# Router logits of twelve FFN tiles from four column tiles of 32, a copy and one product with a fixed 128x8 matrix

## The reference

```python
x = x + xattn(layernorm(x), ctx, ctx, pos, mask, Wq, Wk, Wv, Wo)   # RoPE, masked softmax
# the FFN, on xf = layernorm(x) as 2048 x 512
router_logits = xf @ gate_w.T            # gate_w is 8 x 512
routing = softmax(router_logits, axis=1) # 8 weights for each row
in_scale  = routing @ in_channel_scale   # 8 x 512
out_scale = routing @ out_channel_scale
out = (xf * in_scale) @ sign(weight).T * out_scale + bias
x = x + out
```

## Time and profile before

| | before |
|---|---|
| median of 3 runs | 1149.29 us (1148.65 to 1153.01) |
| the profiled execution, its time | 1149.49 us |
| its span, first to last instruction | 1147.7 us |
| PE busy | 98% of the span |
| PEld, DVE, POOL, ACT busy | 83%, 71%, 62%, 47% |
| granted TensorE clock, mean | 1.000 |

### The profile page before, as it was taken

One profiled execution on the slowest core, in us unless ns is written; L12 is line 12 of the kernel. 1 busy time (PEld: TensorE's weight loads), 2 busy tenths in 40 slices (PEclk: granted clock), 3 DMA queues, 4 the chain that ended last, 5 costly groups with the idle time before them and its releaser, 6 DMA issues.

```text
span 1147.7 us, 22887 instructions
## 1 busy us (share of the span) xinstructions
PE 1130.3 (98%) x7919; PEld 951.8 (83%) x7919; DVE 815.5 (71%) x1363; ACT 537.2 (47%) x1736; POOL 706.1 (62%) x586
## 2 busy tenths in 40 slices
PE   7999999999999999999999999999999999999998
PEld 6778888888888888888888888888888888888876
DVE  5876876767687766877767676677766767776566
ACT  4644444454444454444553435544444544445533
POOL 5855675555667556675665666566675656755544
PEclk9999999999999999999999999999999999999999
DMA  8323332333323222333422323233232232322200
GB/s 233 111 72 114 114 115 82 90 96 94 93 82 102 74 82 85 121 107 92 116 85 68 103 75 90 91 106 107 84 94 73 74 92 65 93 72 83 83 20 37
DMA packets 134339, 105.29 MB, mean 92 GB/s; under 512 B 10664, under 2 KB 108984, under 8 KB 134256
## 3 DMA queue, kind: packets, MB, share of 16 engines
q1 hardware_dynamic: 128848, 93.72, 27.8%
q10 hardware_dynamic: 4640, 8.40, 2.1%
q0 software_dynamic: 768, 2.10, 0.6%
HBM read 100.00 MB, written 4.19 MB: 91 GB/s over the span
## 4 chain that ended last, share of the span: by engine, by line
PE 91%; DVE 3%; issue 2%; DMA 1%; ACT 1%; POOL 1%; SPq 0%; DVEq 0%; ACTq 0%; POOLq 0%
PE chunk L1232 22%; PE chunk L1234 21%; PE chunk L1233 21%; PE duo_ps L1298 6%; PE o_ps L1321 3%; PE duo_ps L1221 2%; PE aux L1221 2%; PE duo_ps L1321 2%; PE chunk L1278 1%; PE o_ps L1280 1%; PE o_ps L1279 1%; PE chunk L1280 1%; PE o_ps L1278 1%; PE chunk L1279 1%; DVE swp L931 1%
## 5 line engine op out<-in xcount | busy, mean ns | idle before, releaser
L448 POOL TENSOR_TENSOR w_lo<-raw,w_hi 128x512 fp32r<-128x512 f32 x192 | 247.8, 1304 | 311.9 <-ACT w_hi L589 311.7
L931 DVE TENSOR_TENSOR swp<-chunk,sinT 64x512 f32<-64x512 f32 x320 | 220.3, 688 | 54.2 <-PE chunk L1234 33.4
L589 ACT ACTIVATE w_hi<-raw 128x512 fp32r<-128x512 f32 x192 | 116.4, 629 | 270.1 <-PE chunk L1234 203.8
L1232 PE MATMUL chunk<-xT_hi,w_hi 128*128 128x512 f32 x512 | 206.7, 404 | 0.6 <-POOL w_lo L448 0.6
L1234 PE MATMUL chunk<-xT_hi,w_lo 128*128 128x512 f32 x512 | 200.3, 391 | 0.0
L1233 PE MATMUL chunk<-xT_lo,w_hi 128*128 128x512 f32 x512 | 199.7, 390 | 0.0
L1232 PE MATMUL chunk<-wo_hi,oT_hi 128*128 128x512 f32 x496 | 196.8, 397 | 1.2 <-DVE oT_lo L865 1.2
L1234 PE MATMUL chunk<-wo_hi,oT_lo 128*128 128x512 f32 x496 | 193.5, 390 | 0.0
L1233 PE MATMUL chunk<-wo_lo,oT_hi 128*128 128x512 f32 x496 | 193.3, 390 | 0.0
L626 ACT ACTIVATE probs<-scores,neg_max 128x64 f32<-128x64 f32 x512 | 170.4, 337 | 41.2 <-DVE neg_max L887 41.2
L455 POOL TENSOR_TENSOR qT<-qT,swp 128x512 f32<-128x512 f32 x128 | 165.2, 1298 | 35.9 <-DVE qT L933 35.5
(11 more groups left out here) (271 smaller groups left out, 2033.5 us busy)
## 6 DMA issues: line engine op xcount, KB each, us to landing
raw<-in_L_xattn_Wq SPq DMA_DIRECT2D x128, 256.0 KB, 2.8
raw<-in_L_xattn_Wo SPq DMA_DIRECT2D x128, 256.0 KB, 2.7
raw<-in_L_xattn_Wk SPq DMA_DIRECT2D x32, 256.0 KB
raw<-in_L_xattn_Wv SPq DMA_DIRECT2D x32, 256.0 KB, 3.0
acc<-in_x ACTq DMA_DIRECT2D x14, 256.0 KB, 7.4
x_tile<-in_x SPq DMA_DIRECT2D x12, 256.0 KB, 2.9
c_tile<-in_ctx SPq DMA_DIRECT2D x12, 256.0 KB, 3.2
result<-y ACTq DMA_DIRECT2D x12, 256.0 KB, 2.0
```

The lines of the kernel that those rows point to most:

```text
L448: nc.gpsimd.tensor_tensor(lo, raw[:, r, :], hi.bitcast(F32), ALU.subtract).then_inc(wsplit_lo, 1)
L589: return nc.scalar.activation(dst, src, ACT.Copy)
L931: last = nc.vector.tensor_tensor(swp[to, k, :], bank[of, :], sinT[to, here], ALU.mult)
L1232: nc.tensor.matmul(bank, a_hi, b_hi, start=i == 0, stop=False)
```

## The change

In the twelve slots `t_logits` is replaced by two steps. `t_partials` makes four products whose stationary operand is 32 columns of the gate matrix (8 of them filled, 24 zeros) and whose moving operand is one 128x128 chunk of the transposed tile; chunk c goes to partitions 32c to 32c+31 of `aux`, so each product has a column tile of its own and none accumulates. ACT copies the 128x128 result to `partT`. `t_sum_partials` then makes one product with `partT` as stationary and the fixed 128x8 matrix `gate_pick` as moving operand, which sums the four partial results and gives the logits in the old layout. `t_partials` stands ahead of `probs_T`, `t_sum_partials` where `t_logits` stood. The copy stands on ACT between the weight splits and `pT_hi_split`. `last_tiles` keeps `t_logits`. At the start DVE sums four 8-column groups of the identity to make `gate_pick`, and ACT's one copy to `gateT` is 128x128 instead of 128x32.

```diff
@@ buffers
-        gateT = sb("gateT", [P, EC, NE])
+        gateT, gate_pick, partT = sb("gateT", [P, EC, 32]), sb("gate_pick", [P, NE]), sb("partT", [P, P])
@@ ScalarE
+            def partial_logits(f, b):
+                act.wait_ge(part_done, f + 1)
+                copy(b.partT, b.bank[:, 0:P]).then_inc(part_ok, 1)
...
                 split_hi(s, 4)
                 if s.odd:
                     split_hi(s, 5)
+                if s.ffn:
+                    partial_logits(f[0], in_slot)
                 pT_hi_split(s, 0)
                 pT_hi_split(s, 1)
...
-                copy(gateT[:, :, :], by_chunk(GATE_BANK)[:, :, 0:NE]).then_inc(gate_ok, 1)
+                copy(gateT[:, :, :], by_chunk(GATE_BANK)[:, :, 0:32]).then_inc(gate_ok, 1)
@@ VectorE, first_positions
+                dve.wait_ge(ident_ok, 2)
+                nc.vector.tensor_reduce(gate_pick[:, :], ident[:, :].rearrange("p (c e) -> p e c", c=EC)[:, 0:NE, :], AX.X, ALU.add).then_inc(pick_ok, 1)
                 dve.wait_ge(pos_in, 16)
@@ TensorE
+            def t_partials(f, b):
+                pe.wait_ge(fn_T, f + 1)
+                for c in range(EC):
+                    last = nc.tensor.matmul(b.bank[32 * c:32 * c + 32, 0:P], gateT[:, c, :], b.tile_T[:, bass.ts(c, P)],
+                                            start=True, stop=True)
+                last.then_inc(part_done, 1)
+
+            def t_sum_partials(f, b):
+                pe.wait_ge(part_ok, f + 1)
+                nc.tensor.matmul(b.bank[:, 0:NE], b.partT, gate_pick[:, :], start=True, stop=True).then_inc(lg_done, 1)
...
                 project(s, 0)
                 if not s.odd:
                     project(s, 1)
+                if s.ffn:
+                    t_partials(f, in_slot)
                 probs_T(s, 0)
                 probs_T(s, 1)
...
                 if s.ffn:
-                    t_logits(f, in_slot)
+                    t_sum_partials(f, in_slot)
                 project(s, 1 if s.odd else 2)
```

More of the change, by code:

```diff
@@ L144, in attention_ffn, with __init__ @@
         class FfnBuffers:
-            def __init__(self, stat, mv, var, rstd, bank, tile, tile_T, route, routeT, rexp, rmax, rsum, rrec, xs_hi, xs_lo, y):
+            def __init__(self, stat, mv, var, rstd, bank, tile, tile_T, route, routeT, rexp, rmax, rsum, rrec, xs_hi, xs_lo, y, partT):
+                self.partT = partT
                 self.stat, self.mv, self.var, self.rstd = stat, mv, var, rstd
@@ L156, in attention_ffn @@
         in_slot = FfnBuffers(f_stat[:, :], f_mv[:, :], f_var[:, :], f_rstd[:, :], aux[:, :], f_tile[:, :], fT[:, :], route[:, :], routeT[:, :], rexp[:, :],
-                             rmax[:, :], rsum[:, :], rrec[:, :], xs_hi[:, :], xs_lo[:, :], y[:, :])
+                             rmax[:, :], rsum[:, :], rrec[:, :], xs_hi[:, :], xs_lo[:, :], y[:, :], partT[:, :])
         at_end = [FfnBuffers(s_stat[:, p, :], s_mv[:, p, :], s_var[:, p:p + 1], s_rstd[:, p:p + 1],
@@ L163, in attention_ffn @@
                              xT_hi[:, p, E:2 * E], xT_lo[:, p, E:2 * E],
-                             (cosT if p < 2 else sinT)[:, bass.ts(p % 2, E)]) for p in range(PAIRS)]
+                             (cosT if p < 2 else sinT)[:, bass.ts(p % 2, E)], None) for p in range(PAIRS)]
         assert QT % 2 == 0
@@ L199, in attention_ffn @@
         fn_tr, fn_T, lg_done, rm_ok, re_ok, rr_ok = (sem(n) for n in ("fn_tr", "fn_T", "lg_done", "rm_ok", "re_ok", "rr_ok"))
+        part_done, part_ok, pick_ok = sem("part_done"), sem("part_ok"), sem("pick_ok")
         rt_ok, rt_tr, rt_hi, rt_lo = (sem(n) for n in ("rt_ok", "rt_tr", "rt_hi", "rt_lo"))
@@ L1374, in t_logits @@
                 for c in range(EC):
-                    last = nc.tensor.matmul(b.bank[:, 0:NE], b.tile_T[:, bass.ts(c, P)], gateT[:, c, :],
+                    last = nc.tensor.matmul(b.bank[:, 0:NE], b.tile_T[:, bass.ts(c, P)], gateT[:, c, 0:NE],
                                             start=c == 0, stop=c == EC - 1)
@@ L1425, in first_attention @@
                 pe.wait_ge(fw_ok, EC)
+                pe.wait_ge(pick_ok, 1)
                 scores_of(s, 0)
```

## The result

The changed kernel took 1155.31 us (median of 13 runs, 1153.07 to 1159.32), the kernel before 1151.75 us (13 runs beside it, 1148.45 to 1155.03). The ratio is 1.004 with an interval of 1.0027 to 1.0053: 0.4% slower, clear of no change. The profiled execution took 1153.49 us over a span of 1151.4 us, at a mean granted clock of 0.999.

What follows compares the result with a forecast made beforehand. PE's stream, waits included, was taken to bound the kernel. Even slots -1.1 and odd slots +4.0 gave +2.9 us: 1152.4 against the profiled 1149.49, 1152.2 us against the median; range 1146.8 to 1155.5.

Steps and rivals of the forecast that it cites:

- sum over the slots, +2.9: All twelve slots: six even ones give -1.1 us, six odd ones +4.0, together +2.9 us.
- PE bound, no cover for what PE issues or waits for: 300 to 1100 us: PE busy 798.69 of 800.00 us, so its added work or waits count one to one.
- Even slots, -0.18 each: Six even slots: new products 0.49 + 0.22 us replace 0.89, copy in time; -0.18 us each, -1.1 in all.
- The partial products, 0.49 us: PE, each slot: two column-tile switches at 0.25 us plus two steps of 0.12, tiles running beside each other.
- program order: Rival: matmuls start strictly in order, so partial products take five steps, 0.85 us; total +5.1, 1154.4 us; chance 0.15.
- tiles in a row: Rival: streams of different data don't overlap, partial products take 1.21 us a slot; total 1156.5 us; chance 0.10.
- Odd slots, a wait of 0.85 and +0.67 each: Six odd slots: PE waits 0.85 us for ACT's copy behind three splits; +0.67 us each, +4.0 in all.
- The rival without a wait in odd slots: ACT finishes the copy early enough, so all twelve slots gain: -2.2 us, 1147.1 us; chance 0.12.
- The +8.0 that the prediction had for a wait in every slot: If the copy were the bottleneck in all twelve slots: 12 x 0.67 = +8.0 us; ACT's idle 2.01 us spoke against it.
- The cover for `pT_hi`: Odd slots: the copy delays `pT_hi` by at most 0.285 us, hidden before `values` loads; uncovered it would cost 0.285.
- the last of the sum: Final call: +2.9 us, 0.25%, lies under the 0.5% (5.7 us) measurement can tell, so "the same"; chance 0.84.

Runs made afterwards that it cites:

- e1: The changed kernel with ACT's copy to `partT` moved, in odd slots, ahead of two weight splits; 1148.50 us, ratio 0.9977 to the kernel before.
- e8: The changed kernel with ACT's copy moved ahead of two weight splits in odd slots, run once more; 1148.75 us, ratio 0.9973 to the kernel before.
- e4: The changed kernel with its four partial products in one column tile, accumulating; 1160.09 us in 4 runs, ratio 1.0071 to the kernel before.
- e5: The kernel before, old logits kept, plus ACT's 128x128 copy to a spare buffer and PE's wait for it; 1161.28 us, ratio 1.0081 to the kernel before.
- e2: The kernel before with only the edits at the start (`gate_pick` reduction, larger `gateT` copy, PE's wait); 1152.45 us, ratio 1.0003 to the kernel before.
- e3: The changed kernel with DVE's `gate_pick` reduction moved from its first instruction to the first slot's end; 1156.53 us, ratio 1.0028 to the kernel before.

## Why the prediction was wrong

It said 1152.2 us and "the same"; it is 1155.3 us and slower by 0.4%, clear of no change. Its sum over the slots, +2.9, was right to 0.1 us; its call was not.

- **PE bound, no cover for what PE issues or waits for:** right. +2.81 us in the slots moves the time at equal clock by 1.9 to 3.0, -2.04 us in e1 and e8 by -1.5 to -2.2.
- **Even slots, -0.18 each:** -0.17 each. The summing product took 348.08 - 347.86 = 0.22 us, as said.
- **The partial products, 0.49 us:** 0.50. From the last projection's load to the transposes' pass 347.03 - 346.14 = 0.89 us where it was 345.10 - 344.88 = 0.22, and the eight transposes then take 347.86 - 347.03 = 0.83 where they took 1.00: 0.67 - 0.17 = 0.50. (The 0.89 itself was forecast as 0.7; the transposes give the difference back.) Of the rivals, program order wanted 0.85 and tiles in a row 1.21. The timeline cut at 346.75 us has four of the eight records started within 0.07 us:

```profile
346.68 0.32 PE L1386 MATMUL aux<-c_tile,gateT 128*32 128x128 f32 x4
```

  Read one by one they start 0, 7, 13 and 20 ns after the first, and the other four from 133 ns on: one step of 0.13 us is seen where 0.12 was taken. In e4, with one column tile, no two start closer than 0.109 us. So streams of different data do run beside each other, and e4 shows what it costs when they go in a row: 0.50 + 0.64 = 1.14 us. How the rest of the 0.50 divides between the second step and the two switches, no run shows. The Trainium skill has matmuls start and end in program order (TensorE: Matmul & The Clock Gate, Part 3); whether the eight records do so the trace does not show, since it does not name the product of a record.
- **Odd slots, a wait of 0.85 and +0.67 each:** 0.81 and +0.64. With no wait the summing load comes 347.86 - 346.68 = 1.18 us after the first partial load, here 385.35 - 383.36 = 1.99. (The waits' view lists 3.3 us for the six, since it counts from the modelled end of the last record; the load's own bracket says 0.78.) The copy took 0.26 in the odd slots (0.28 in the even ones) where 0.285 was taken from the earlier trace rows, and the release 385.35 - 385.30 = 0.05. e1 shows the cause: the copy's place in ACT's order. The rival without a wait in odd slots fell as its argument against said: the first split can't start before PE's projection is done. What neither saw is that the copy need not wait for all three splits. The rule of the Trainium skill in TensorEngine Tiling (Array Packing), section Performance Considerations, that the evacuation may become the bottleneck, holds for the odd slots and for no even one. The +8.0 that the prediction had for a wait in every slot did not come; that e5 costs 7.9 is chance, six waits of 1.31 and not twelve of 0.67.
- **The cover for `pT_hi`:** held. DVE's second `pT_lo` and the load of `values` behind it (before):

```profile
386.50 0.68 DVE L873 TENSOR_TENSOR pT_lo<-duo_ps,pT_hi 128x512 fp32r<-128x512 f32 x1
```

```profile
388.55 0.19 PEld L1331 LDWEIGHTS o_ps<-pT_hi,v_hi 64*128 64x128 f32 x2 [0.35 <-issue]
```

  `pT_lo` ends at 387.18, 1.37 us ahead of its reader. DVE's reduction and the larger `gateT` copy cost nothing that e2 could tell, to within some 2 us.
- **The step that failed is the last of the sum:** "About 0.5% (5.7 us) is what a measurement of this kernel can tell from no change, so this is 'the same'". The 13 runs beside each other told 0.4% from no change, with an interval of 0.13% to either side; two later sets told 0.29 and 0.25%. The bound was taken without asking how far single runs scatter (1148.65 to 1153.01 in the three of before, 4.4 us) and that their median over a dozen is known much better.
- **Terms were missing, too.** The sum was made on an execution at clock 1.000 (1149.49 us), which 16 of the 93 runs of before have; their median is 1151.63. That is 1151.63 - 1149.29 = 2.34 us of the 3.1 between 1152.2 and 1155.31, and without it the time would be below the 1155.0 from which the prediction counted "slower". It moves both kernels and no ratio. The 0.3 us outside the span and a clock that is lower by 0.001, about 1 us, are part of the 0.4%; the cause of either stays open.

## What to carry to other kernels

Where a small step on the full engine is cut in two with another engine's copy between, its price is set less by the two pieces than by what stands ahead of the copy in the other engine's order: here 0.17 us were won in each slot, and 0.81 lost in those where two further splits came first. Look up in the trace when that engine is free, and put the copy there: one moved call turned +0.25 to 0.4% into -0.25% (e1, e8). And before calling a sum of 0.25% "no change", see how much the median of a dozen runs scatters, and at what clock the execution ran on which the sum is made.

## What the runs showed of the hardware

Four fp32 products in column tiles of 32, each with different moving data, show as eight records, of which four start within 20 ns and the other four 133 ns behind them. In one column tile (e4) the eight start one by one, 0.109 to 0.134 us apart.

In e5 TensorE fell to half its clock in the middle of the program, behind three of its six waits. Two of the waiting loads, and the windows around them:

```profile
740.65 0.97 PEld L1382 LDWEIGHTS aux<-gateT,c_tile 128*128 128x128 f32 x8 [1.29 <-ACT partT L590]
948.20 0.97 PEld L1382 LDWEIGHTS aux<-gateT,c_tile 128*128 128x128 f32 x8 [1.29 <-ACT partT L590]
```

```profile
736.00:742.20 6.20, 5.15 (x32) 4.31 (x31) 2.57 (x6) 3.05 (x8) 2.72 (x3) 1.00 0.06 10
742.20:745.60 3.40, 3.40 (x10) 2.63 (x9) 3.08 (x6) 0.11 (x2) 1.08 (x2) 0.50 0.82 269
944.00:950.40 6.40, 5.35 (x33) 4.46 (x32) 2.78 (x8) 3.16 (x8) 3.38 (x3) 1.00 0.10 36
950.40:953.80 3.40, 3.40 (x12) 2.27 (x12) 2.47 (x4) 0.29 (x1) 1.08 (x2) 0.50 0.57 167
```

The clock is 1.00 up to 1.4 to 2.2 us behind the wait, then 0.50 for 3.4 us with PE busy throughout. Read from slot to slot, e5's waits are 1.31 us long; behind those of 0.81 us, six in each trace of the changed kernel and of e3, the clock stayed at 1.00, and no other trace has half clock in the middle of the program. Near its start or end every profiled execution but the first of before has such a stretch, of 3.4 or 6.8 us. So a wait of PE may cost more than its length. But this rests on one execution: another run of e5 had a mean clock of 1.000 (1156.97 us), and why three of the six and not the others, these runs don't show.
